# Value products of a local attention: two heads' turned probabilities as weights, values streamed beside zeros

## The chip, the cores and the metric

One core of a Trainium2 chip. The metric is the device time of one execution in microseconds: 4424.85 us in the median of three runs (4423.68 to 4428.69).

## The reference, cut to what matters

The layer has two branches, whose outputs are added: a delta-rule attention (not touched), and a transformer of six layers on 16 sequences of 256 tokens with 128 channels. A layer of the transformer is local attention and a gated feed-forward block:

```python
DIM = 128; DEPTH = 6; HEADS = 16; DIM_HEAD = 64; WINDOW = 32

def local_attention(q, k, v):
    # windows of 32 queries, each against its own and the preceding window's keys
    bk2, bv2 = look(bk), look(bv)                      # (b, h, 8, 64, 64)
    sim = jnp.einsum('bhwie,bhwje->bhwij', bq, bk2) * QK_SCALE
    sim = jnp.where(mask, -jnp.finfo(sim.dtype).max, sim)
    attn = jax.nn.softmax(sim, -1)                     # 32 queries x 64 keys
    out = jnp.einsum('bhwij,bhwje->bhwie', attn, bv2)  # the value products
    return out.reshape(b, h, n, d)
# attn_layer: q, k, v = x @ Wqkv; l2norm and rotary on q, k; local_attention; @ Wo
# ffn_layer: layernorm; a, gate = split(x @ W1 + b1); (a * gelu(gate)) @ W2 + b2
```

Everything is float32. The sequences are independent of each other; within one, a layer needs the layer before.

## The kernel before, in words

`local_transformer` is a software pipeline written out by hand. A body is one pass of it and works on five sequences (items) at once, each a stage further: `new` (projection of queries and keys, 8 chunks), `turn` (scaling, transposes to head-major form, the value projection), `att` (scores, softmax, first value products), `out` (last value products, output projection, layer norm statistics) and `ffn`. 16 bodies make a layer, 96 the transformer, and four more empty it. Each engine has its own `body(b)`: the list of calls there is the order in which that engine executes, and semaphores (`need(engine, semaphore, count)`) hold it to its inputs and to the buffers that come free. An engine never goes past a call that waits. There is no planner: to move work is to move a line of such a list.

- The state is kept turned (channels on partitions, tokens in columns). A projection is three float32r products of 512 columns (`project`, L1402) into the one bank `ps_proj`; VectorE rotates it (L1228, L1235), ScalarE squares it (`square`, L1066), and the next projection waits for that square. GpSimd adds and scales, TensorE transposes (`turn_qk`, L1437).
- `score(x, k)` handles 8 heads of one half of the sequence (128 tokens): a mask product (L1448), then 32 products of a 64-row by 32-column weight with 64 streamed columns (L1454). In float32 each product is two records.
- `turn_probs` transposes the normalised probabilities (L1469). `pT` then has, for two heads r, 64 keys each on the partitions and the queries in the columns.
- `weigh(x, k)` (L1487) makes the value products: for 4 pairs of heads, 4 windows and 2 heads, a 64 x 64 block of values is the weight and the 32 columns of that head's probabilities are streamed. The result is already turned (value channel on partitions), and ScalarE copies it into `oT` (`heads_out`, L1115), from which `join_heads` makes the output projection.
- The values: `value(b, x, n)` projects four parts into `ps_p`, ScalarE copies them into `v` (`value_out`, L1088; tokens on partitions, one buffer). A window needs its own keys and those of the window before on one set of 64 partitions. `window(x)` on SP (L935) therefore copies `v` into `vw`, inside SBUF, with 16 DMAs a sequence, after the fourth part is in `v`. `vw` has two buffers. `value_out` of the next sequence's part 0 waits until all 16 have landed, since it overwrites `v`.
- The layer norm of `ffn` shares VectorE's Newton steps for the inverse square roots with `turn`'s norms (`inverse_roots`), at the start of a body.

Of the kernel before, what the change touches and what calls it, by code (L numbers as in the profile page):

```python
# [11 lines left out]
ALU = mybir.AluOpType  # L12
# [15 lines left out]
UNITS = 4  # L28
NNORM = 64
NPREP = 10  # L30
# [770 lines left out]
def local_transformer(nc, stateT, ident, wqkv_d, scales_d, wb_d, par_d, rot_d, mask_d):  # L801
# [8 lines left out]
    with ExitStack() as stack:  # L810
        def sb(name, shape, dt=F32):
# [18 lines left out]
        ident_r = sb("ident_r", [P, P], F32R)  # L830
# [15 lines left out]
        vw = sb("vw", [P, 2, NWIN, INNER // 2])  # L846
# [5 lines left out]
        oT = sb("oT", [P, 2, NPAIR, L])  # L852
# [5 lines left out]
        hid = sb("hid", [P, FCH, L])  # L858
# [9 lines left out]
            "vw_in0", "vw_in1",  # L868
            "scored", "maxed", "shifted", "exped", "p_summed", "reciped", "normed", "p_turned", "p_turned_out",
            "valued", "values_out", "wo_done", "x_added", "xf_ready", "mean_done", "centred",  # L870
# [36 lines left out]

        block = stack.enter_context(nc.Block())

        @block.sync  # L910
        def _(sp):
            sp.dma_start(par_all[:, :], par_d).then_inc(S["loaded_const"], 16)
            sp.dma_start(rot_base[:, :, :], rot_d.rearrange("(u p) n -> p u n", p=P)).then_inc(S["loaded_const"], 16)
            sp.dma_start(hid[:, :, :].rearrange("p c t -> p (c t)")[:, 0:2 * KEYS], mask_d).then_inc(S["loaded_const"], 16)
# [8 lines left out]
            def window(x):  # L923

                if not x.there:
                    return
                need(sp, S["v_out"], x.u * 4 + 4)
                for r in range(2):
                    for a in range(2):
                        rows = slice(r * KEYS + a * WIN, r * KEYS + (a + 1) * WIN)  # L930
                        cols = slice(r * CK, (r + 1) * CK)
                        for c in range(4):
                            n = 1 if a == 0 and c == 3 else 2
                            w = c + 1 - a
                            sp.dma_start(vw[rows, x.q, w:w + 4 * (n - 1) + 1:4, :], v[c * WIN:(c + 1) * WIN, 0:n, cols])\  # L935
                                .then_inc(S[f"vw_in{x.q}"], 16)

            def body(b):
                new, turn, att, out, ffn = b.items
                window(att)  # L940
# [8 lines left out]
            load_wqkv(0)  # L949
            pipeline(body)  # L950

        @block.gpsimd
        def _(pool):

            nc.gpsimd.memset(kT[:, :, :, 0:WIN], 0.0).then_inc(S["prepared"], 1)
            nc.gpsimd.memset(vw[:, :, 0, :], 0.0).then_inc(S["prepared"], 1)
# [6 lines left out]
            nc.gpsimd.tensor_copy(ident_r[:, :], ident[:, :]).then_inc(S["prepared"], 1)  # L963

            pool.wait_ge(S["loaded_const"], 48)
            nc.gpsimd.tensor_copy(mask[:, :, :], hid[:, :, :].rearrange("p c t -> p (c t)")[:, 0:2 * KEYS]
# [42 lines left out]
            def body(b):  # L1009
                new, turn, att, out, ffn = b.items  # L1010
                if turn.there:
# [3 lines left out]
                scale(att, 7)  # L1015
                scale(turn, 0)
                scale(turn, 1)
                add(turn, 7)
                add(new, 0)
                scale(turn, 2)  # L1020
                add(new, 1)
                scale(turn, 3)
                norm(out, 3)
                scale(turn, 4)
                add(new, 2)
                norm(att, 0)
                add(new, 3)
                norm(att, 1)
                scale(turn, 5)
                add(new, 4)  # L1030
                add(new, 5)
                norm(att, 2)
                scale(turn, 6)
                add(new, 6)
# [4 lines left out]
        def _(act):  # L1039
# [41 lines left out]
            def value_out(x, before, n):  # L1081
# [4 lines left out]
                if n == 0:  # L1086
                    need(act, S[f"vw_in{before.q}"], 256 * (before.h + 1))
# [20 lines left out]

            def heads_out(x, k):

                if not x.there:
                    return
                half, e = unit(k)
                need(act, S["valued"], x.u * 4 + (k + 1))
                nc.scalar.activation(oT[:, x.q, 4 * e:4 * e + 4, half * P:(half + 1) * P],  # L1115
                                     ps_o[:, :].rearrange("p (c t) -> p c t", c=4), ACT.Copy).then_inc(S["values_out"], 1)
# [34 lines left out]
            def body(b):  # L1151
                new, turn, att, out, ffn = b.items
                shift_state(ffn)
                square(turn, 6)
                heads_out(out, 0)
                probs_out(out, 1)
                turned_out(att, 5)
                square_centred(ffn)
                value_out(att, out, 3)
                if b.switch == -1:  # L1160
                    convert(b, (4, 5), (S["v_projected"], turn.u * 4))
                square(turn, 7)
# [8 lines left out]
                turned_out(att, 6)  # L1171
                heads_out(out, 1)
                probs_out(out, 2)
                turned_out(att, 7)
                square(new, 0)
                turned_out(turn, 0)
                heads_out(out, 2)
# [6 lines left out]
                square(new, 2)  # L1184
                value_out(turn, att, 0)
                probs_out(out, 3)
                exp(att, 0)
                square(new, 3)
                turned_out(turn, 3)
                exp(att, 1)  # L1190
                heads_out(out, 3)
                value_out(turn, att, 1)
                turned_out(turn, 4)
                square(new, 4)
                probs_out(att, 0)
                square(new, 5)
                exp(att, 2)
                value_out(turn, att, 2)
                if b.switch == 1:
                    need(act, S["y_done"], ffn.u + 1)  # L1200
                    nc.scalar.activation(w1[:, :, :, :].rearrange("p a c n -> p (a c n)"), stage_w1, ACT.Copy)\
                        .then_inc(S["conv_act"], 1)

# [3 lines left out]
        def _(dve):  # L1207
            dve.wait_ge(S["loaded_const"], 48)
# [101 lines left out]
            def hidden(x):  # L1310
# [5 lines left out]
                for c, bank in enumerate((ps_g[:, L:2 * L], ps_c[:, 0:L], ps_c[:, L:2 * L])):  # L1316
                    nc.vector.scalar_tensor_tensor(hid[:, c, :], bank, par[:, c:c + 1], gate[:, c, :], ALU.add, ALU.mult)\
# [10 lines left out]
            def body(b):  # L1328
                new, turn, att, out, ffn = b.items
                centre(ffn)  # L1330
                rotate(turn, 7, 0)
                rotate(turn, 7, 1)
                sum_squares(turn, 7)
                inverse_roots(turn, ffn)
# [10 lines left out]
                top(out, 3)  # L1345
                rotate(new, 0, 1)
                if b.switch == -1:
                    convert(b, (4, 5), 4)
                deviate(ffn)
                shift(out, 3)  # L1350
                sum_squares(new, 0)
                rotate(new, 1, 0)
                rotate(new, 1, 1)
                total(out, 3)
                sum_squares(new, 1)
                top(att, 0)
                rotate(new, 2, 0)
                shift(att, 0)
                rotate(new, 2, 1)
                top(att, 1)  # L1360
                hidden(ffn)
                rotate(new, 3, 0)
                sum_squares(new, 2)
                rotate(new, 3, 1)
                shift(att, 1)
                total(att, 0)
                sum_squares(new, 3)
                rotate(new, 4, 0)
# [8 lines left out]
                total(att, 1)  # L1377
# [3 lines left out]
                top(att, 2)  # L1381
                shift(att, 2)
# [7 lines left out]
                sum_squares(new, 6)  # L1390

# [3 lines left out]
        def _(pe):  # L1395
# [77 lines left out]
            def weigh(x, k):  # L1473
# [5 lines left out]
                need(pe, S["values_out"], x.u * 4 + k)  # L1479
                if k == 0:  # L1480
                    need(pe, S[f"vw_in{x.q}"], 256 * (x.h + 1))
                for c in range(NPAIR // 2):
                    for w in range(4):
                        for r in range(2):
                            rows = slice(r * KEYS, (r + 1) * KEYS)
                            first = (4 * e + c) * DH
                            mm = nc.tensor.matmul(ps_o[rows, c * P + w * WIN:c * P + (w + 1) * WIN],  # L1487
                                                  vw[rows, x.q, 4 * half + w, first:first + DH],
                                                  pT[rows, k % 2, c, w * WIN:(w + 1) * WIN],
                                                  start=True, stop=True, skip_group_check=True)  # L1490
                mm.then_inc(S["valued"], 1)

            def join_heads(b, x):
# [7 lines left out]
                for c in range(NPAIR):  # L1501
                    mm = nc.tensor.matmul(ps_c[:, 0:L], wo[:, c, :], oT[:, x.q, c, :], start=c == 0, stop=c == NPAIR - 1)  # L1502
# [29 lines left out]
            def ffn_in(x, part):  # L1532
# [3 lines left out]
                need(pe, S["xn_ready"], x.u + 1)  # L1536
                if part == 2:
# [6 lines left out]
            def ffn_out(x):  # L1544
# [4 lines left out]
                for c in range(FCH):  # L1549
                    mm = nc.tensor.matmul(ps_c[:, 0:L], w2[:, c, :], hid[:, c, :], start=c == 0, stop=c == FCH - 1)  # L1550
                mm.then_inc(S["y_done"], 1)

            def body(b):
                new, turn, att, out, ffn = b.items
                query_key(b, new, 0)
                turn_qk(att, 7)
                weigh(out, 2)
                spread(ffn)
                turn_qk(turn, 0)
                score(att, 0)  # L1560
                query_key(b, new, 1)
                turn_qk(turn, 1)
                ffn_in(ffn, 0)
                ffn_in(ffn, 1)
                value(b, turn, 0)
                query_key(b, new, 2)
                turn_qk(turn, 2)
                score(att, 1)
                ffn_in(ffn, 2)
                turn_qk(turn, 3)  # L1570
                query_key(b, new, 3)
                turn_probs(out, 3, turn, 0)
                ffn_out(ffn)
                weigh(out, 3)
                query_key(b, new, 4)
                value(b, turn, 1)
                turn_qk(turn, 4)
                score(att, 2)
                turn_probs(att, 0, turn, 1)
                query_key(b, new, 5)  # L1580
                join_heads(b, out)
                turn_qk(turn, 5)
                query_key(b, new, 6)
                value(b, turn, 2)
                weigh(att, 0)
                turn_probs(att, 1, turn, 2)
# [3 lines left out]
                mean(out)  # L1590
                query_key(b, new, 7)
                value(b, turn, 3)
                variance(out)
                turn_qk(turn, 6)
                turn_probs(att, 2, turn, 3)
                weigh(att, 1)
                score(att, 3)
# [148 lines left out]
```

## Time and profile before

| | |
|---|---|
| median of three runs | 4424.85 us |
| the profiled execution | 4430.44 us, span 4428.3 us |
| PE / weight loads, share of the span | 90% / 76% |
| VectorE / ScalarE / GpSimd | 77% / 56% / 52% |
| mean granted clock of TensorE | 0.929 |
| the transformer | from about 725 us to 4409 us |

"PE" is TensorE's products, "PEld" its weight loads, DVE VectorE, ACT ScalarE, POOL GpSimd, SP the engine that issues the DMAs. A row of windows has the stretch, its length, and the busy us (and instructions) of PE, PEld, DVE, ACT and POOL, then TensorE's granted clock, the busy share of the 16 DMA engines, and GB/s. The time before 725 us is the other branch, which the change leaves alone. Busy shares of the whole span mix it in; a layer or a body of the transformer says more.

### The profile page before, as it was taken

To read this page: it belongs to the slowest core of one execution; us is meant where nothing else is said; L and a number is where in the kernel's file an instruction comes from. 1 tells how busy PE (TensorE), PEld (TensorE's weight loads), DVE (VectorE), ACT (ScalarE), POOL (GpSimd) and SP (SyncE) were. 2 spreads that over 40 slices of the span, in tenths; PEclk is the share of its full clock that TensorE was granted. 3 is DMA by queue.
4 is the path that set the end of the run, shared out by engine and by line. 5 is a ranking of instruction groups with operands and counts; after the bars stand their busy time and mean duration, and the time that the engine had idled before them with its cause. 6 is when DMAs were issued, how large, how long until landed. Compare 5 with 4: busy or idle time off the path is not lost. (4 is left out here: it accounts for less than half of the span.)

```text
span 4428.3 us, 165233 instructions
## 1 busy us (share of the span) xinstructions
PE 4003.8 (90%) x71312; PEld 3348.1 (76%) x71312; DVE 3420.2 (77%) x6567; ACT 2492.3 (56%) x4423; POOL 2303.8 (52%) x2141
## 2 busy tenths in 40 slices
PE   4746743899999999999999999999999999999997
PEld 4635531688888888878888888888788888888885
DVE  4376565788888888888888888888888888888883
ACT  2322211466666666666666666666666666666663
POOL 1000002566656666666666666666666665666661
PEclk9766655899999999999999999999999999999998
DMA  1000000222222222222222222222222222222222
GB/s 57 22 12 12 2 12 34 71 56 56 56 56 57 71 56 57 56 57 71 56 56 56 56 66 71 56 56 56 66 71 56 56 56 53 64 55 57 53 57 64
DMA packets 133868, 232.99 MB, mean 53 GB/s; under 512 B 26640, under 2 KB 36624, under 8 KB 131472
## 3 DMA queue, kind: packets, MB, share of 16 engines
q1 hardware_dynamic: 133136, 222.32, 20.6%
q8 instruction: 571, 9.36, 1.0%
q14 instruction: 161, 1.32, 0.1%
HBM read 29.28 MB, written 4.19 MB: 8 GB/s over the span
## 5 line engine op out<-in xcount | busy, mean ns | idle before, releaser
L987 POOL TENSOR_TENSOR qk<-rot_a,rot_b 128x512 f32<-128x512 f32 x768 | 983.5, 1285 | 418.7 <-PE bank L1437 378.2
L997 POOL TENSOR_TENSOR qk<-qk,rn 128x512 f32<-128x512 f32 x768 | 801.5, 1049 | 216.0 <-DVE rn L69 206.1
L1487 PEld LDWEIGHTS bank<-pT,vw 64*64 64x64 f32 x24576 | 752.3, 136 | 100.5 <-issue 99.5
L1487 PE MATMUL bank<-pT,vw 64*64 64x32 f32 x24576 | 794.9, 220 | 0.7 <-ACT pT L1106 0.7
L1006 POOL TENSOR_TENSOR pr<-pr,prec 128x512 f32<-128x512 f32 x384 | 400.2, 1042 | 706.1 <-DVE prec L1272 705.9
L1228 DVE TENSOR_TENSOR rot_a<-bank,rot 128x512 f32<-128x512 f32 x768 | 529.4, 689 | 297.6 <-PE bank L1402 296.4
L1066 ACT ACTIVATE sq<-bank 128x512 f32<-128x512 f32 x768 | 457.5, 596 | 470.4 <-DVE rot_b L1235 465.0
L1402 PE MATMUL bank<-w_hi,xs_hi 128*128 128x512 f32 x1152 | 555.3, 482 | 77.7 <-ACT sq L1066 28.2
L1243 DVE TENSOR_REDUCE ss<-sq 128x8 f32<-128x512 f32 x768 | 509.6, 664 | 139.0 <-ACT sq L1066 139.0
L1235 DVE TENSOR_TENSOR rot_b<-bank,rot 128x512 f32<-128x512 f32 x768 | 522.9, 681 | 0.0
L1437 PE MATMUL bank<-ident,qk 128*128 128x128 f32 x3072 | 472.6, 277 | 4.9 <-POOL qk L997 4.7
L1402 PE MATMUL bank<-w_hi,xs_lo 128*128 128x512 f32 x1152 | 461.8, 401 | 0.0
L1402 PE MATMUL bank<-w_lo,xs_hi 128*128 128x512 f32 x1152 | 460.5, 400 | 0.0
L1454 PEld LDWEIGHTS bank<-kT,qT 64*32 64x32 f32 x24576 | 363.5, 107 | 116.8 <-issue 116.7
L1437 PEld LDWEIGHTS bank<-ident,qk 128*128 128x128 f32 x3072 | 386.1, 145 | 81.5 <-POOL qk L997 9.3
L1454 PE MATMUL bank<-kT,qT 64*32 64x64 f32 x24576 | 426.9, 219 | 1.2 <-issue 0.9
L1088 ACT ACTIVATE v<-bank 128x512 f32<-128x512 f32 x384 | 229.1, 597 | 278.3 <-PE bank L1402 274.2
L1502 PE MATMUL bank<-oT,wo 128*128 128x256 f32 x1536 | 347.2, 379 | 0.7 <-ACT oT L1115 0.7
L1106 ACT ACTIVATE pT<-bank 128x512 f32<-128x512 f32 x384 | 229.2, 597 | 192.2 <-PE bank L1469 192.2
L1077 ACT ACTIVATE kT<-bank 128x512 f32<-128x512 f32 x384 | 228.1, 594 | 191.9 <-PE bank L1437 191.2
L1402 PEld LDWEIGHTS bank<-w_hi,xs_hi 128*128 128x128 f32 x1152 | 221.2, 192 | 137.0 <-issue 52.1
L1502 PEld LDWEIGHTS bank<-oT,wo 128*128 128x128 f32 x1536 | 291.5, 190 | 43.3 <-ACT oT L1115 0.8
(238 smaller groups left out, 6724.6 us busy)
## 6 DMA issues: line engine op xcount, KB each, us to landing
vw<-v SPq DMA_DIRECT2D x1344, 128.0 KB
vw<-v SPq DMA_DIRECT2D x192, 64.0 KB
stage<-in_wqkv SPq DMA_DIRECT2D x6, 1536.0 KB, 6.1
stage<-in_wb_all SPq DMA_DIRECT2D x6, 1088.0 KB, 5.3
d_band<-in_band SPq DMA_DIRECT2D x8, 512.0 KB, 5.3
d_xt<-in_x SPq DMA_DIRECT2D x4, 512.0 KB, 4.1
base_scratch<-d_res SPq DMA_DIRECT2D x4, 512.0 KB, 3.0
o_base<-base_scratch SPq DMA_DIRECT2D x1, 2048.0 KB, 8.4
```

The costliest lines, as they stand in the source:

```text
L987: nc.gpsimd.tensor_tensor(qk[:, c, :], rot_a[:, c % 2, :], rot_b[:, c % 2, :], ALU.add)\
L997: nc.gpsimd.tensor_tensor(y, y, rn[:, x.q, 8 * c:8 * c + 8].unsqueeze(2).to_broadcast([P, 8, DH]), ALU.mult).then_inc(S["scaled"], 1)
L1006: nc.gpsimd.tensor_tensor(y, y, prec[:, k % 2, :].unsqueeze(2).to_broadcast([P, NPAIR, KEYS]), ALU.mult).then_inc(S["normed"], 1)
L1066: nc.scalar.activation(sq[:, :], ps_proj[:, :], ACT.Square).then_inc(S["squared"], 1)
L1228: nc.vector.tensor_tensor(rot_a[:, c % 2, :].rearrange("p (h d) -> p h d", h=8), ps_proj[:, :].rearrange("p (h d) -> p h d", h=8), cos, AL ...
L1235: nc.vector.tensor_tensor(rot_b[:, c % 2, :].rearrange("p (h a d) -> p h a d", h=8, a=2), y[:, :, ::-1, :], sin, ALU.mult).then_inc(S["rot ...
L1243: nc.vector.tensor_reduce(ss[:, 8 * c:8 * c + 8], sq[:, :].rearrange("p (h d) -> p h d", h=8), AX.X, ALU.add).then_inc(S["summed"], 1)
L1402: mm = nc.tensor.matmul(out[:, :], x[:, q, half * P:(half + 1) * P], w[:, cols:cols + CK], start=n == 0, stop=n == 2)
L1437: mm = nc.tensor.transpose(ps_turn[:, i * P:(i + 1) * P], qk[:, c, i * P:(i + 1) * P], ident[:, :])
L1454: mm = nc.tensor.matmul(bank[w * WIN:(w + 1) * WIN, h * KEYS:(h + 1) * KEYS], qT[rows, x.q, h, q0:q0 + WIN], kT[rows, x.q, h, q0:q0 + KEYS ...
L1487: mm = nc.tensor.matmul(ps_o[rows, c * P + w * WIN:c * P + (w + 1) * WIN], vw[rows, x.q, 4 * half + w, first:first + DH], pT[rows, k % 2, ...
L1502: mm = nc.tensor.matmul(ps_c[:, 0:L], wo[:, c, :], oT[:, x.q, c, :], start=c == 0, stop=c == NPAIR - 1)
```

## The change

The value products swap their operands. The turned probabilities of two heads (128 partitions, 32 queries) become the weight, and the values of the two heads are streamed, 128 columns: head 0's values stand in the first 64 columns on the first 64 partitions, head 1's in the last 64 on the other 64, and the rest of `vw` is zero, written once by VectorE. A product gives 32 queries by two heads of 64 channels; the four windows go to the four groups of 32 output partitions. There are 16 products a call and not 32. The output now has tokens on partitions: ScalarE copies it to `o_tok` (`heads_taken`), TensorE transposes it into `ps_g` (`turn_heads`, four transposes a call, four calls a sequence), ScalarE copies that to `oT` (`heads_out`).

`vw` becomes a ring of three halves. `window(x, half)` issues 14 DMAs for the first half and 16 for the second, each of 32 partitions by 2 KB. It is called for `turn`, no longer for `att`: the first half waits for v's second part, the second for v's fourth and for the products that read the slot before. `value_out(turn, att, 0)` waits for both halves of `att`.

All five orders are written anew. `inverse_roots`, `centre`, `shift_state` and `square_centred` move to the end of the body before, `score(x, 0)` too. `oT` has one buffer, `hid` is written in place of `gate`.

```diff
+SLOTS = 3
+HALF_DMAS = (14, 16)
-        vw = sb("vw", [P, 2, NWIN, INNER // 2])
+        vw = sb("vw", [P, SLOTS, NWIN // 2, 2, CK])
-        oT = sb("oT", [P, 2, NPAIR, L])
+        o_tok = sb("o_tok", [P, CK])
+        oT = sb("oT", [P, NPAIR, L])
+        def slot(x, half):
+            return (2 * x.u + half) % SLOTS
@@ SP
-            def window(x):
+            def window(x, half):
-                need(sp, S["v_out"], x.u * 4 + 4)
+                need(sp, S["v_out"], x.u * 4 + 2 * half + 2)
+                need(sp, S["valued"], x.u * 4 + 2 * half - 4)
                 for r in range(2):
                     for a in range(2):
                         rows = slice(r * KEYS + a * WIN, r * KEYS + (a + 1) * WIN)
                         cols = slice(r * CK, (r + 1) * CK)
-                        for c in range(4):
-                            n = 1 if a == 0 and c == 3 else 2
-                            w = c + 1 - a
-                            sp.dma_start(vw[rows, x.q, w:w + 4 * (n - 1) + 1:4, :], v[c * WIN:(c + 1) * WIN, 0:n, cols])
+                        for w in range(4):
+                            n, c = (half, w) if a == 1 else (half, w - 1) if w else (half - 1, 3)
+                            if n >= 0:
+                                sp.dma_start(vw[rows, slot(x, half), w, r, :], v[c * WIN:(c + 1) * WIN, n, cols])
-                window(att)
+                window(turn, 0)
+                window(turn, 1)
@@ ScalarE, its body up to square(new, 3), without the layer switches
+                high_half(b, new)
+                value_out(att, out, 3)
+                probs_out(out, 2)
+                heads_taken(out, 1)
+                turned_out(att, 7)
+                heads_taken(out, 2)
+                heads_out(out, 1)
+                square(new, 0)
+                turned_out(turn, 0)
+                affine(ffn)
+                exp(out, 3)
+                heads_out(out, 2)
+                value_out(turn, att, 0)
+                turned_out(turn, 1)
+                square(new, 1)
+                gelu(ffn)
+                square(new, 2)
...
@@ VectorE
+            nc.vector.memset(vw[:, :, :, :, :], 0.0).then_inc(S["vw_zeroed"], 1)
@@ TensorE
-                        for r in range(2):
-                            rows = slice(r * KEYS, (r + 1) * KEYS)
-                            first = (4 * e + c) * DH
-                            mm = nc.tensor.matmul(ps_o[rows, c * P + w * WIN:c * P + (w + 1) * WIN],
-                                                  vw[rows, x.q, 4 * half + w, first:first + DH],
-                                                  pT[rows, k % 2, c, w * WIN:(w + 1) * WIN],
+                        first = (4 * e + c) * DH
+                        mm = nc.tensor.matmul(ps_o[w * WIN:(w + 1) * WIN, c * P:(c + 1) * P].rearrange("p (r d) -> p r d", r=2),
+                                              pT[:, k % 2, c, w * WIN:(w + 1) * WIN],
+                                              vw[:, slot(x, half), w, :, first:first + DH],
+            def turn_heads(x, k):
+                need(pe, S["o_out"], x.u * 4 + (k + 1))
+                need(pe, S["values_out"], x.u * 4 + k)
+                if k == 3:
+                    need(pe, S["hid_done"], (x.u - 1) * 3 + 1)
+                for c in range(NPAIR // 2):
+                    mm = nc.tensor.transpose(ps_g[:, c * P:(c + 1) * P], o_tok[:, c * P:(c + 1) * P], ident[:, :])
@@ TensorE, the new order of its body, calls of one line joined
+                query_key(b, new, 0); turn_heads(out, 1); weigh(out, 2); spread(ffn); value(b, turn, 0)
+                turn_qk(turn, 0); turn_heads(out, 2); query_key(b, new, 1); score(att, 1); turn_qk(turn, 1)
+                ffn_in(ffn, 1); ffn_in(ffn, 0); query_key(b, new, 2); turn_qk(turn, 2)
+                turn_probs(out, 3, turn, 0); score(att, 2); ffn_in(ffn, 2); query_key(b, new, 3)
+                value(b, turn, 1); turn_qk(turn, 3); ffn_out(ffn); weigh(out, 3); turn_qk(turn, 4)
+                query_key(b, new, 4); turn_probs(att, 0, turn, 1); turn_qk(turn, 5); turn_heads(out, 3)
+                weigh(att, 0); query_key(b, new, 5); join_heads(b, out); query_key(b, new, 6)
+                value(b, turn, 2); turn_heads(att, 0); mean(out); turn_qk(turn, 6)
+                turn_probs(att, 1, turn, 2); query_key(b, new, 7); score(att, 3); value(b, turn, 3)
+                variance(out); turn_qk(turn, 7); weigh(att, 1); turn_probs(att, 2, turn, 3); score(turn, 0)
```

## Rows read from the trace of the kernel before

**Rows 1.** Windows: a layer, then one body; columns as told above.
```profile
2058.00:2646.00 588.00, 582.72 (x10153) 490.26 (x10146) 489.75 (x953) 381.09 (x685) 375.26 (x349) 0.99 0.26 61
2406.19:2442.99 36.80, 36.80 (x646) 31.04 (x645) 30.65 (x61) 24.01 (x43) 23.55 (x22) 1.00 0.25 59
```
**Rows 2.** Groups by shape: line, engine, tile, shapes, count, then busy us, mean ns.
```profile
L1487 PE MATMUL bank<-pT,vw 64*64 64x32 f32 x24576 | 794.9, 220 | 0.7 <-ACT pT L1106 0.7
L1454 PE MATMUL bank<-kT,qT 64*32 64x64 f32 x24576 | 426.9, 219 | 1.2 <-issue 0.9
```
**Rows 3.** Timeline of TensorE in one body: start us, us, line.
```profile
2408.65 0.71 PE L1527 MATMUL bank<-ident,rn 128*128 128x128 f32 x4
2409.20 0.60 PE L1437 MATMUL bank<-ident,qk 128*128 128x128 f32 x4
...
2412.21 1.89 PE L1541 MATMUL bank<-xn,w 128*128 128x256 f32 x8
2413.75 0.58 PE L1402 MATMUL bank<-w_hi,xs_hi 128*128 128x512 f32 x1
...
2436.60 0.40 PE L1402 MATMUL bank<-w_hi,xs_hi 128*128 128x512 f32 x1
...
2437.29 0.57 PE L1518 MATMUL bank<-mean_w,xsq 128*128 128x1 f32 x4
2437.72 0.63 PE L1437 MATMUL bank<-ident,qk 128*128 128x128 f32 x4
2438.24 0.63 PE L1469 MATMUL bank<-ident,pr 128*128 128x128 f32 x4
2438.79 2.06 PE L1487 MATMUL bank<-pT,vw 64*64 64x32 f32 x64
2440.78 0.39 PE L1448 MATMUL bank<-mask,ident_b 128*128 128x512 bf16 x1
2441.10 1.10 PE L1454 MATMUL bank<-kT,qT 64*32 64x64 f32 x64
2442.13 0.50 PE L1402 MATMUL bank<-w_hi,xs_hi 128*128 128x512 f32 x1
```
**Rows 4.** Timeline of ScalarE: v's part 3, a square, and v's next part 0.
```profile
2400.70 0.60 ACT L1088 ACTIVATE v<-bank 128x512 f32<-128x512 f32 x1 [0.29 <-PE bank L1402]
...
2409.69 0.60 ACT L1066 ACTIVATE sq<-bank 128x512 f32<-128x512 f32 x1 [2.32 <-DVE rot_b L1235]
...
2417.94 0.59 ACT L1088 ACTIVATE v<-bank 128x512 f32<-128x512 f32 x1
```
**Rows 5.** SP's issues at L935, duration ns min/median/max: the whole run, then one burst.
```profile
L935 SPq DMA_DIRECT2D vw<-v x1536: 585/598/2278, 793.7 to 4352.4; - x192
...
L935 SPq DMA_DIRECT2D vw<-v x16: 586/598/1617, 2401.3 to 2412.6; - x16
```
**Rows 6.** DMA issues by size, whole run.
```profile
vw<-v SPq DMA_DIRECT2D x192, 64.0 KB
```
**Rows 7.** Window: the last microsecond of that burst.
```profile
2415.00:2416.00 1.00, 1.00 (x8) 0.62 (x6) 0.71 (x2) 0.99 (x4) 1.00 (x2) 1.00 0.07 16
```
**Rows 8.** Timeline of VectorE: the last Newton step of a body.
```profile
2407.63 0.23 DVE L69 SCALAR_TENSOR_TENSOR rn<-rn_t,rn 128x66 f32<-128x66 f32 x1
```
**Rows 9.** Timeline of TensorE where a layer changes.
```profile
1319.47 0.77 PE L1402 MATMUL bank<-w_hi,xs_hi 128*128 128x512 f32 x1 [4.45 <-issue]
```
**Rows 10.** Windows around two changes of layer.
```profile
1315.00:1320.00 5.00, 0.55 (x4) 0.50 (x2) 4.90 (x7) 0.95 (x2) 4.42 (x5) 0.57 0.68 157
1320.00:1325.00 5.00, 5.00 (x67) 4.33 (x65) 3.82 (x6) 1.19 (x2) 1.54 (x2) 0.50 0.60 137
1325.00:1330.00 5.00, 5.00 (x85) 4.17 (x84) 1.61 (x3) 2.21 (x4) 2.27 (x2) 0.56 0.01 3
...
2520.00:2525.00 5.00, 4.75 (x67) 4.05 (x67) 4.61 (x7) 0.95 (x2) 2.32 (x2) 0.60 0.72 167
```
**Rows 11.** Waits, whole run: who waited for whom, us in total, times, longest.
```profile
PE bank L1402 <- issue: 18.2, 5, 4.5
```

More of the change, by code:

```diff
@@ L906, in unit, with landed @@
             return k // 2, k % 2
+        def slot(x, half):
+            return (2 * x.u + half) % SLOTS
+        def landed(x, half):
+            k = 2 * x.u + half
+            return 16 * sum(HALF_DMAS[i % 2] for i in range(k % SLOTS, k + 1, SLOTS))
         block = stack.enter_context(nc.Block())
@@ L1010, in body @@
                 new, turn, att, out, ffn = b.items
-                if turn.there:
+                if out.there:
+                    low_half(new, "normed", out.u * 4 + 3)
+                elif att.there:
+                    low_half(new, "scaled", att.u * 8 + 8)
+                elif turn.there:
                     low_half(new, "added", turn.u * 8 + 7)
@@ L1014, in body @@
                     low_half(new, "prepared", NPREP)
-                scale(att, 7)
                 scale(turn, 0)
+                add(turn, 7)
                 scale(turn, 1)
-                add(turn, 7)
                 add(new, 0)
+                norm(out, 3)
                 scale(turn, 2)
+                scale(turn, 3)
                 add(new, 1)
-                scale(turn, 3)
-                norm(out, 3)
                 scale(turn, 4)
+                scale(turn, 5)
                 add(new, 2)
@@ L1027, in body @@
                 add(new, 3)
-                norm(att, 1)
-                scale(turn, 5)
                 add(new, 4)
                 add(new, 5)
+                scale(turn, 6)
+                norm(att, 1)
+                add(new, 6)
+                scale(turn, 7)
                 norm(att, 2)
-                scale(turn, 6)
-                add(new, 6)
             pipeline(body)
@@ L1085, in value_out @@
                 need(act, S["v_projected"], x.u * 4 + (n + 1))
-                if n == 0:
-                    need(act, S[f"vw_in{before.q}"], 256 * (before.h + 1))
+                if n == 0 and before.there:
+                    need(act, S[f"vw_in{slot(before, 0)}"], landed(before, 0))
+                    need(act, S[f"vw_in{slot(before, 1)}"], landed(before, 1))
                 nc.scalar.activation(v[:, n // 2, n % 2 * CK:(n % 2 + 1) * CK], ps_p[:, :], ACT.Copy)\
@@ L1107, in probs_out, with heads_taken @@
                     .then_inc(S["p_turned_out"], 1)
+            def heads_taken(x, k):
+                if not x.there:
+                    return
+                need(act, S["valued"], x.u * 4 + (k + 1))
+                need(act, S["o_turned"], x.u * 4 + k)
+                nc.scalar.activation(o_tok[:, :], ps_o[:, :], ACT.Copy).then_inc(S["o_out"], 1)
             def heads_out(x, k):
@@ L1113, in heads_out @@
                 half, e = unit(k)
[L1114 to L1116 removed]
+                need(act, S["o_turned"], x.u * 4 + (k + 1))
+                nc.scalar.activation(oT[:, 4 * e:4 * e + 4, half * P:(half + 1) * P],
+                                     ps_g[:, :].rearrange("p (c t) -> p c t", c=4), ACT.Copy).then_inc(S["values_out"], 1)
             def shift_state(x):
@@ L1152, in body @@
                 new, turn, att, out, ffn = b.items
[L1153 to L1162, printed above, removed]
                 if b.switch == -2:
@@ L1182, in body @@
                 gelu(ffn)
+                square(new, 2)
                 turned_out(turn, 2)
-                square(new, 2)
-                value_out(turn, att, 0)
                 probs_out(out, 3)
                 exp(att, 0)
+                turned_out(turn, 3)
+                value_out(turn, att, 1)
                 square(new, 3)
-                turned_out(turn, 3)
-                exp(att, 1)
[L1191 to L1195, printed above, removed]
+                turned_out(turn, 4)
+                heads_taken(out, 3)
+                probs_out(att, 0)
+                square(new, 4)
+                heads_out(out, 3)
+                exp(att, 1)
+                exp(att, 2)
                 square(new, 5)
-                exp(att, 2)
+                turned_out(turn, 5)
+                heads_taken(att, 0)
+                shift_state(out)
                 value_out(turn, att, 2)
@@ L1202, in body @@
                         .then_inc(S["conv_act"], 1)
+                square(new, 6)
+                probs_out(att, 1)
+                heads_out(att, 0)
+                square_centred(out)
+                turned_out(turn, 6)
+                square(new, 7)
             pipeline(body)
@@ L1344, in body @@
                 rotate(new, 0, 0)
-                top(out, 3)
+                shift(out, 3)
                 rotate(new, 0, 1)
@@ L1380, in body @@
                 rotate(new, 5, 1)
-                top(att, 2)
-                shift(att, 2)
+                total(att, 1)
                 sum_squares(new, 5)
@@ L1390, in body @@
                 sum_squares(new, 6)
+                centre(out)
+                rotate(new, 7, 0)
+                rotate(new, 7, 1)
+                top(att, 3)
+                sum_squares(new, 7)
+                inverse_roots(new, out)
             pipeline(body)
@@ L1536, in ffn_in @@
                 need(pe, S["xn_ready"], x.u + 1)
+                if part == 0:
+                    need(pe, S["values_out"], min(x.u * 4 + 7, UNITS * NSEQ * DEPTH))
                 if part == 2:
@@ L1549, in ffn_out @@
                 for c in range(FCH):
-                    mm = nc.tensor.matmul(ps_c[:, 0:L], w2[:, c, :], hid[:, c, :], start=c == 0, stop=c == FCH - 1)
+                    mm = nc.tensor.matmul(ps_c[:, 0:L], w2[:, c, :], gate[:, c, :], start=c == 0, stop=c == FCH - 1)
                 mm.then_inc(S["y_done"], 1)
@@ L1555, in body @@
                 query_key(b, new, 0)
-                turn_qk(att, 7)
+                turn_heads(out, 1)
                 weigh(out, 2)
                 spread(ffn)
+                value(b, turn, 0)
                 turn_qk(turn, 0)
-                score(att, 0)
+                turn_heads(out, 2)
                 query_key(b, new, 1)
+                score(att, 1)
                 turn_qk(turn, 1)
+                ffn_in(ffn, 1)
                 ffn_in(ffn, 0)
-                ffn_in(ffn, 1)
-                value(b, turn, 0)
                 query_key(b, new, 2)
                 turn_qk(turn, 2)
-                score(att, 1)
+                turn_probs(out, 3, turn, 0)
+                score(att, 2)
                 ffn_in(ffn, 2)
+                query_key(b, new, 3)
+                value(b, turn, 1)
                 turn_qk(turn, 3)
-                query_key(b, new, 3)
-                turn_probs(out, 3, turn, 0)
                 ffn_out(ffn)
                 weigh(out, 3)
+                turn_qk(turn, 4)
                 query_key(b, new, 4)
-                value(b, turn, 1)
-                turn_qk(turn, 4)
-                score(att, 2)
                 turn_probs(att, 0, turn, 1)
+                turn_qk(turn, 5)
+                turn_heads(out, 3)
+                weigh(att, 0)
                 query_key(b, new, 5)
                 join_heads(b, out)
-                turn_qk(turn, 5)
                 query_key(b, new, 6)
                 value(b, turn, 2)
-                weigh(att, 0)
-                turn_probs(att, 1, turn, 2)
+                turn_heads(att, 0)
                 if b.switch == 1:
@@ L1590, in body @@
                 mean(out)
+                turn_qk(turn, 6)
+                turn_probs(att, 1, turn, 2)
                 query_key(b, new, 7)
+                score(att, 3)
                 value(b, turn, 3)
                 variance(out)
-                turn_qk(turn, 6)
+                turn_qk(turn, 7)
+                weigh(att, 1)
                 turn_probs(att, 2, turn, 3)
-                weigh(att, 1)
-                score(att, 3)
+                score(turn, 0)
             pipeline(body)
```

63 lines of the change are left out of this document (28 added, 35 removed).

## Prediction

> **What bounds the kernel now.** I read the windows first. A layer of 588 us has TensorE busy for 582.7 us, and one body of the pipeline, 36.80 us, has it busy without a break, with VectorE at 30.65, ScalarE at 24.01 and GpSimd at 23.55 us [rows 1]. So in the transformer TensorE's written order sets the pace, and an edit there is worth what it does to a body, times 96 (16 sequences, 6 layers). Next the groups by shape: the value products are 24,576 records (each fp32 product is two), with 795 us on PE [rows 2]. Then TensorE's own timeline of a body, for what each block takes from its start to the next one's: weigh 1.99 us, the mask and the score products 0.32 + 1.03, a group of four transposes 0.52 or 0.55 (I take 0.5), value 0.69, variance 0.43, spread 0.55, the two first feed-forward calls 1.54 [rows 3]. Last the queue of SP, because each body copies v into vw: ScalarE finishes v's fourth part at 2401.30, SP starts its 16 issues at once, the last starts at 2412.6, and in the window 2415 to 2416 the DMA engines are nearly quiet (share 0.07). The burst takes 13.8 us. ScalarE overwrites v at 2417.94, so 16.6 us were allowed and nothing waited [rows 4, 5, 7]. That is a cover of 2.8 us which no list of waits shows.
>
> **TensorE's work.** A weigh is now 32 records with 32-column weights (a window's probabilities of two heads) and 128 streamed columns. The nearest row is the score: 64 records, 32-column weights, 64 streamed columns, four column positions, 1.03 us. Both stream 4,096 columns, so 1.03 again, 1.05 with the change of tiles. Saved: 4 x (1.99 - 1.05) = 3.8 us a body. Added are four turn_heads of four transposes, 4 x 0.5 = 2.0 us. A body falls from 36.8 to 35.0 us if TensorE stays the bound. Bounds for a weigh: 1.0 (as the score), and 4.3, if nothing overlaps: 32 x (0.11 to stream 128 columns, as the variance's four 128-column loads stand 0.11 apart and four 128-column transposes 0.13, + 0.03 for a load of 32).
>
> The row of the score shows what decides here: its 64 loads and products all use one half of the rows, differ only in their column position, and take 1.03 us, 16 ns each, where one 64-column stream alone needs about 54 (half of 0.11). The loads and streams of four column positions therefore run beside each other. The Trainium skill ("TensorE: Matmul & The Clock Gate", Part 3: Packing small matmuls) says that a weight load overlaps products in flight only when the row group differs. By that, the new weigh, which uses all rows each time, would be serial. The trace speaks against the rule.
>
> **ScalarE and VectorE.** heads_taken adds four copies of 0.60 us a body: 24.0 + 2.4 = 26.4 of 35.0, hidden beside TensorE. VectorE keeps its work: 30.65 of 35.0. The new order puts inverse_roots at the end of its body. Its chain from the last projection to the last Newton step ended at 2407.86, 0.8 us before spread [rows 3, 8]. In the new order TensorE passes score 3, value, variance, turn, weigh, turn, score 0, projection, turn_heads and weigh in between: 1.35 + 0.7 + 0.43 + 0.5 + 1.05 + 0.5 + 1.35 + 0.7 + 0.5 + 1.05 = 8.1 us, against the chain's 7.9. Hidden, barely; some tenths a body if late. hid folded into gate, oT with one buffer, the waits for ps_g (values_out, hid_done): I walked the order, and the awaited copies come some tenths ahead; zero. VectorE's memset of vw, 12,288 columns (a 512-column pass takes 0.69), is at most 14 us once beside the load of the weights; zero, at most 3 us.
>
> **The copies of v, where the gain is lost.** window is moved to the item `turn`, and split in halves of 14 and 16 DMAs of 64 KB. The first half leaves in mid-body; it has a body of time. The second waits for v_out of part 3, which ScalarE does early in the next body, and for weigh(att, 1). Behind it stands ScalarE's value_out(turn, att, 0), which overwrites v, and in ScalarE's queue behind that turned_out(turn, 1) and square(new, 1). query_key(new, 2) on TensorE needs that square.
>
> What TensorE has to do between the end of weigh(att, 1) and query_key 2: turn_probs 0.5, score 1.35, projection 0.7, turn_heads 0.5, weigh 1.05, spread 0.55, value 0.7, turn 0.5, turn_heads 0.5, projection 0.7, score 1.35, turn 0.5, feed-forward 1.55 = 10.45 us. What the other way takes: 16 issues and the landing, then three ScalarE operations of 0.60 with their handovers, 1.85, and 0.05 to start.
> - The burst's bounds: the issue of a vw DMA takes 598 ns in the median and never under 585, among 1,536 of which 192 move 64 KB [rows 5, 6]. Halving the bytes doesn't make it cheaper. The floor is 15 x 0.6 = 9.0 us plus the 2.5 from the last issue to quiet, 11.5. The top is 13.8, as now; the excess is single issues of up to 2.3 us. Whether these come by the count or the bytes the trace doesn't say, so I take the middle, 13.0.
> - TensorE's gap before query_key 2: 13.0 + 1.9 - 10.45 = 4.4 us (2.9 to 5.2). The body is 35.0 + 4.4 = 39.4 us, or 37.9 to 40.2: at either end over 36.8. The same 16 issues as before stand behind the last part of v, but the order now allows them 10 us and not 16.6.
>
> **The clock.** Where a layer changes, TensorE stands still for up to 4.45 us (18.2 us in five gaps). With the gap that ends at 1319.47 the granted clock falls to half (0.57 over 1315 to 1320), is 0.50 for the next five, 0.56 over 1325 to 1330: 9.9 us of cold work. In 2520 to 2525 it is 0.60, some 3.8 us of work [rows 9 to 11]. The middle is 6.8 us, which lose half of it, 3.4. A gap of 4.4 us in each body is of that size. I take it that three bodies in four pay: 2.6 us. A body is then 42.0 us.
>
> **Sum.** (42.0 - 36.8) x 96 = +499 us. The profiled execution took 4430.4 us (span 4428.3 and 2.1 around it), 5.6 over the runs' median, 4424.85. 4430 + 499 - 5.6 = 4924, say 4925 us.
>
> **Rivals.**
> - *The gap comes but the clock holds.* The gaps shown stand at layer changes only, and a body may differ. (39.4 - 36.8) x 96 = +250: 4675 us.
> - *The copies are in time, the kernel is faster.* If the bytes decide, half of them land in half of 13.8, 6.9 us, against an allowance of 10.45 - 1.9 = 8.5. TensorE stays the bound: (35.0 - 36.8) x 96 = -173: 4252 us. It decides from a burst under 10.3 us (gap under 1.8), issues of 0.52. For it: every added piece fits under TensorE. Against: the 64 KB issues [rows 5, 6]. The Trainium skill ("DMA: Bandwidth & Descriptors", Issuing engines are not separate DMA queues) calls the sequencer's time to start a DMA usually small relative to the DMA. Here the issues are 11.3 of 13.8 us, so this case's rows contradict it.
> - *Between them:* a burst near 10.3, within some per cent of 4425 either way.
> - *The new products don't overlap:* 4.3 us a weigh, TensorE 35.0 + 4 x 3.25 = 48.0; one of them lies in the burst's cover (13.7), which leaves a gap of 1.2: 49.2 us, +1190: 5610 us. The score's row speaks against it.
>
> **Chances.** Forecast 0.45, clock holds 0.30, in time 0.16, between 0.05 (of it 0.01 faster, 0.02 same, 0.02 slower), no overlap 0.04. Within 0.2% (9 us) is what a measurement here can't tell from no change. Faster 0.17, same 0.02, slower 0.81. The range leaves out "in time" and "no overlap": below, 4400; above, every body cold (42.8 us, 5001) and the gap at 5.2 (+0.8 x 96 = 77), about 5090. Slower alone, it is 4530 (floor of the burst, warm clock: +1.1 x 96) to 5090.
>
> **What would show it.** A wait of ScalarE's v on the vw DMAs of some 4 us in every body; TensorE's gap before the projection behind the feed-forward pair; SP's 30 issues a body at a median near 598 ns; a granted clock well under 0.99 over a layer; weigh near 1.05 us. Wrong, if issues of the new form take 0.5 us or less, if the landing follows the bytes, or if ScalarE gets to value_out more than 13 us after weigh(att, 1) for a reason of its own, since then the copies cost nothing extra.

## The result and the profile after

4744.54 us in the median of four runs (4728.2 to 4751.3) against 4426.77 us, the median of four runs of the kernel before; the ratio is 1.0712 (95% interval 1.0683 to 1.0742). The change makes the kernel 7% slower, though TensorE has less to do. The profiled execution took 4728.20 us with a span of 4726.1: 297.8 us more than before, 3.1 us for each of 96 bodies.

Windows of the changed kernel: the stretch of a layer, and one body; the columns are those of [rows 1].

```profile
2055.00:2680.00 625.00, 558.19 (x8166) 450.69 (x8165) 463.72 (x928) 403.71 (x732) 365.35 (x340) 0.95 0.21 54
2403.61:2445.35 41.74, 36.50 (x536) 29.36 (x534) 29.70 (x61) 25.93 (x47) 23.58 (x23) 0.92 0.20 49
```

TensorE was busy without a break in the body of [rows 1]. Here it stands still for 5.24 of the body's 41.74 us. Its timeline, as [rows 3]:

```profile
2407.46 1.08 PE L1514 MATMUL bank<-vw,pT 128*32 128x128 f32 x32
2408.47 0.66 PE L1498 MATMUL bank<-ident,pr 128*128 128x128 f32 x4
...
2417.32 1.89 PE L1582 MATMUL bank<-xn,w 128*128 128x256 f32 x8
2424.46 0.79 PE L1431 MATMUL bank<-w_hi,xs_hi 128*128 128x512 f32 x1 [5.24 <-ACT sq L1081]
```

The new weigh (the first line) takes 1.01 us to the next block, where the old one took 1.99. The gap stands before query_key 2, behind the feed-forward pair, and what ends it is a square on ScalarE. ScalarE's timeline, as [rows 4]:

```profile
2407.68 0.60 ACT L1104 ACTIVATE v<-bank 128x512 f32<-128x512 f32 x1
...
2422.83 0.60 ACT L1104 ACTIVATE v<-bank 128x512 f32<-128x512 f32 x1 [6.06 <-DMA vw<-v]
2423.32 0.59 ACT L1092 ACTIVATE kT<-bank 128x512 f32<-128x512 f32 x1
2423.80 0.60 ACT L1081 ACTIVATE sq<-bank 128x512 f32<-128x512 f32 x1
```

v's part 3 is there at 2408.28, and the block behind weigh(att, 1) starts at 2408.47. Both are what the second half's copies wait for. Yet v is overwritten only at 2422.83, 14.4 us later. In [rows 4] the same copy waited for nothing. The square that TensorE needs is two places behind it. Over the whole run these two are the longest waits of their engines (us, times, longest):

```profile
ACT v L1104 <- DMA vw<-v: 437.5, 95, 6.5
...
PE bank L1431 <- ACT sq L1081: 383.4, 107, 6.0
```

SP's issues, as [rows 5]:

```profile
L946 SPq DMA_DIRECT2D vw<-v x2880: 507/591/2059, 774.6 to 4650.9; - x192
DMA to landing us min/median/max: 1.9/2.0/3.5
```

All 2,880 move 64 KB, and the median issue takes 591 ns, where 598 ns was the median with mostly 128 KB. Half the bytes buy 7 ns. The granted clock around the gap, in windows as in [rows 10]:

```profile
2415.00:2419.00 4.00, 4.00 (x80) 3.05 (x78) 3.35 (x7) 1.74 (x4) 2.71 (x3) 1.00 0.36 87
2419.20:2424.50 5.30, 0.06 (x2) 0.05 (x1) 0.06 (x1) 1.65 (x4) 4.39 (x5) 0.71 0.20 51
2424.50:2430.00 5.50, 5.50 (x80) 4.31 (x81) 3.19 (x5) 4.93 (x8) 1.27 (x1) 0.66 0.00 0
```

It is full (1.00, 2.4 GHz) up to the gap and falls in it. The 0.66 over the 5.5 us behind the gap means 3.7 us at 1.2 GHz. Of 95 bodies, 79 have such a stretch within 12 us behind the gap, and the layer's mean is 0.95 where it was 0.99.

### The profile page after: what moved, and what is told of

Same layout as the page of the kernel before. It is cut to its first block and busy times, and to the rows that moved or that the text cites. A ratio compares the mean times of both kernels' runs of the same rounds, so it can differ in the third digit from the quotient of the medians.

```text
span 4726.1 us, 146508 instructions
## 1 busy us (share of the span) xinstructions
PE 3936.3 (83%) x60560; PEld 3171.3 (67%) x60560; DVE 3352.1 (71%) x6568; ACT 2672.4 (57%) x4807; POOL 2302.0 (49%) x2139
## 5 line engine op out<-in xcount | busy, mean ns | idle before, releaser
L1431 PE MATMUL bank<-w_hi,xs_hi 128*128 128x512 f32 x1152 | 585.3, 508 | 425.7 <-ACT sq L1081 383.4
L1466 PE MATMUL bank<-ident,qk 128*128 128x128 f32 x3072 | 507.7, 291 | 8.3 <-ACT kT L1092 6.0
L1431 PE MATMUL bank<-w_lo,xs_hi 128*128 128x512 f32 x1152 | 474.3, 412 | 0.0
L1483 PEld LDWEIGHTS bank<-kT,qT 64*32 64x32 f32 x24576 | 388.6, 113 | 125.8 <-issue 125.8
L1431 PE MATMUL bank<-w_hi,xs_lo 128*128 128x512 f32 x1152 | 471.6, 409 | 0.0
L1483 PE MATMUL bank<-kT,qT 64*32 64x64 f32 x24576 | 451.7, 226 | 0.0
L1514 PE MATMUL bank<-vw,pT 128*32 128x128 f32 x12288 | 417.9, 277 | 0.2 <-ACT pT L1122 0.2
L1514 PEld LDWEIGHTS bank<-vw,pT 128*32 128x32 f32 x12288 | 314.1, 110 | 81.3 <-issue 64.5
L1131 ACT ACTIVATE o_tok<-bank 128x512 f32<-128x512 f32 x384 | 229.1, 597 | 214.9 <-PE bank L1514 214.9
```

The costliest lines, as they stand in the source:

```text
L1431: mm = nc.tensor.matmul(out[:, :], x[:, q, half * P:(half + 1) * P], w[:, cols:cols + CK], start=n == 0, stop=n == 2)
L1466: mm = nc.tensor.transpose(ps_turn[:, i * P:(i + 1) * P], qk[:, c, i * P:(i + 1) * P], ident[:, :])
L1483: mm = nc.tensor.matmul(bank[w * WIN:(w + 1) * WIN, h * KEYS:(h + 1) * KEYS], qT[rows, x.q, h, q0:q0 + WIN], kT[rows, x.q, h, q0:q0 + KEYS ...
L1514: mm = nc.tensor.matmul(ps_o[w * WIN:(w + 1) * WIN, c * P:(c + 1) * P].rearrange("p (r d) -> p r d", r=2), pT[:, k % 2, c, w * WIN:(w + 1) ...
```

## The experiments

**Two buffers for v.** If the wait for the burst of copies costs the time, a second buffer must give it back: part 0 of the next sequence then goes into the other half of `v` and waits for the copies of the sequence before last. To make room, the DMA scratch is set to 1024 bytes. All else stays.

```diff
-        v = sb("v", [P, 2, INNER])
+        v = sb("v", [P, 2, 2, INNER])                        # by the sequence's parity
...                                                           (v[:, x.q, ...] where v is written and read)
-                if n == 0 and before.there:                   # both halves of x.u - 1
+                if n == 0 and before.there and before.u > 0:  # both halves of x.u - 2
+                    for k in (2 * x.u - 4, 2 * x.u - 3):
+                        need(act, S[f"vw_in{k % SLOTS}"], 16 * sum(...))   # sum cut
-... dynamic_dma_scratch_size=8192)
+... dynamic_dma_scratch_size=1024)
```

> The changed kernel with v in two buffers (by the sequence's parity), so that value_out(turn, att, 0) waits for the copies of the sequence before last. Theory (the second half's burst of 16 issues holds v, and through square(new, 1) TensorE): ScalarE's wait on the vw DMAs goes, TensorE's gap of 3.8 us goes, the clock stays full; a body takes 34.6 to 35.0 us: 4220 to 4260 us. Rival (the swapped products, the transposes behind them or the new order cost the time themselves): it stays above 4600 us, with the gap at another place.

Measured: 4196.09 us, ratio to the kernel before 0.9468 (0.9451 to 0.9486). This version beats both kernels. Its body:

```profile
2442.00:2476.10 34.10, 34.10 (x532) 28.06 (x532) 30.04 (x61) 25.88 (x47) 23.14 (x23) 1.00 0.22 54
```

TensorE has no idle time in it, and the clock is full. From one mean(out) to the next (2463.34 to 2497.80) are 34.46 us, where [rows 1] has 36.80. So the swapped products, the transposes and the new order together are worth 2.34 us a body, and the changed kernel loses all of that and more by having one buffer. A control with the scratch alone:

> A control for the kernel with two buffers of v, which also asks for 1024 bytes of DMA scratch and not 8192 to make room: the changed kernel with that edit alone. Theory: no DMA of this kernel goes through it; 4728 to 4751 us. Rival (the scratch was part of the gain): under 4700.

Measured: 4721.34 us. That is one run, 7 us under the lowest of the changed kernel and just outside what was expected. The gaps are there as before, so the scratch has no part worth naming in the 548 us between one buffer and two.

**Half the DMAs, half the bytes, twice the DMAs.** These three vary the count of the issues and the bytes. In the first, `for r in range(2 - half)`: the 8 copies of head row 1 are left out of a second half. In the second, each copy of a second half takes only `0:CK // 2` of its columns, and the rest of the values isn't copied. In the third, each copy of a second half is issued as two of half the columns.

> The changed kernel with 8 of the 16 DMAs of a second half left out (those of head row 1; part of the values stays zero), each still 64 KB. Theory by issues: 8 x 0.6 + 2.5 = 7.3 us, under the 8.5 that are allowed; the gap goes, 4220 to 4280 us. Theory by bytes: half the bytes, also in time, 4220 to 4280. Neither: about 4740 us.

> The changed kernel with all 16 DMAs of a second half, each of 32 KB and not 64 (half of the values' columns isn't copied). Theory by issues: 16 x 0.6 + 2.3 = 11.9 us or more, gap 2.8 to 3.5 us; 4640 to 4745 us. Theory by bytes: half the burst, the gap goes, 4220 to 4280 us.

> The changed kernel with each DMA of a second half split into two of half the columns: 32 issues for the same bytes. Theory by issues: 16 more x 0.6 = 9.6 us more in each body's gap (13.4 us), and no less cold work behind it: 5650 to 5900 us. Theory by bytes: as the changed kernel, about 4740 us.

Measured: 4200.88, 4719.65 and 5748.18 us, one run each. With 8 issues, ScalarE's copies into v waited 1.5 us for DMAs in the whole run. Its waits in the second and third:

```profile
ACT v L1105 <- DMA vw<-v: 404.2, 95, 6.1
```
```profile
ACT v L1106 <- DMA vw<-v: 1372.8, 95, 16.9
```

8 issues are in time. 16 are late even with half the bytes (4.3 us a body, where the changed kernel has 4.6). 16 more issues for the same bytes cost ScalarE 9.8 us a body more, 0.61 us each. So it is the count of the issues that limits the burst, and the theory by bytes is out.

**Filling the gap.** The gap costs twice, by itself and by the halved clock behind it. Products whose result nobody reads keep TensorE busy in part of the gap and so show the second cost alone.

```diff
                 ffn_in(ffn, 0)
+                filler(out)   # 12 bf16 products of 512 columns into ps_o, after o_out of k = 2
                 query_key(b, new, 2)
```

> The changed kernel with 12 idle products more in each body, bf16, 512 columns, into the bank ps_o, which is free there, right before query_key(new, 2), where TensorE stands still for 3.8 us: 12 x 0.22 = 2.6 us of work nobody reads. Theory (the gap costs twice, once by itself and once by the halved clock behind it, 3.5 us of cold work a body, half of it lost): the rest of the gap, 1.2 us, leaves the clock up; 1.8 us a body less, about 4575 us (4560 to 4620). Rival (cold work lies in another wait's shadow): 4740 us, or above where a gap was under 2.6 us.

Measured: 4613.80 us (4599.9 to 4618.6), ratio to before 1.0414 (1.0388 to 1.0440). With 12 more products in each body the kernel is 131 us faster than the changed one. In the same stretch the clock is now full, and TensorE's idle time before the projection is down from 383.4 us:

```profile
2055.00:2680.00 625.00, 596.22 (x8690) 468.11 (x8689) 482.87 (x967) 417.64 (x760) 375.96 (x350) 1.00 0.22 57
```
```profile
PE bank L1432 <- ACT sq L1082: 151.2, 103, 6.3
```

So the halved clock costs 1.4 us a body at the least (6 of 95 bodies had a gap under 2.6 us, and in those the filler itself costs). The gain of 1.8 us that was expected was a little too high.

**Moving the wait** instead of removing it.

```diff
@@ ScalarE
                 heads_out(out, 2)
-                value_out(turn, att, 0)
                 turned_out(turn, 1)
...
                 turned_out(turn, 2)
+                value_out(turn, att, 0)
@@ TensorE
-                turn_probs(out, 3, turn, 0)
                 score(att, 2)
                 ffn_in(ffn, 2)
+                turn_probs(out, 3, turn, 0)
```

> The changed kernel with one buffer of v as it is; only two calls move: value_out(turn, att, 0) on ScalarE goes from before turned_out(turn, 1) to behind turned_out(turn, 2), and turn_probs(out, 3) on TensorE from before score(att, 2) to behind ffn_in(ffn, 2). Theory (what costs is the place of value_out, 10.6 us of TensorE's work behind the burst's start where 14.5 are needed): query_key 2 and 3, their transposes, a score and the feed-forward call come into the cover, 3.4 us more; the gap falls to 0 to 0.8 us, the clock stays up; 4200 to 4290 us. Rival (SP's burst costs wherever the wait stands): 4700 or more.

Measured: 4356.01 us, ratio to before 0.9837 (0.9814 to 0.9860): faster than both kernels with v in one buffer, but 66 us above the range expected. ScalarE no longer waits for the copies (7.1 us in all). In their place TensorE has two waits of half a microsecond in each body:

```profile
PE bank L1591 <- DVE gate L1346: 53.5, 95, 2.0
PE bank L1498 <- ACT v L1104: 53.3, 106, 2.9
```

This idle time is 1.1 us a body, and the kernel stands 1.7 us a body above the one with two buffers. Measured from the start of one block to the start of the next, the two places cost 0.69 and 0.71 us in the body at 2400 us, which is most of the 1.7. The first wait is that of the feed-forward's last product for its input; why that input is late is not traced. The second follows from the edit: `turn_probs(out, 3)` writes the bank from which `value_out(turn, att, 0)` copies, so it waits for the very copy that was moved back.

**Two queues.** ScalarE issues the 8 DMAs of head row 1 behind its value_out(att, out, 3).

```diff
+                copy_row_1(att)    # nc.scalar.dma_start x8, after v_out of part 3 and weigh(att, 1)
```

> The changed kernel, v in one buffer, with the second half's burst shared: SP issues the 8 DMAs of head row 0, ScalarE the 8 of head row 1, right behind its value_out(att, out, 3). The copies are in time either way (8 x 0.6 + 2.5 = 7.3 us). If an issue holds ScalarE as it holds SP (0.6 us), 4.8 us stand before probs_out(out, 2) and heads_taken(out, 1), for which TensorE has some 1.5 us; it stands still there for 2 to 3 us a body: 4430 to 4600 us. If an issue costs ScalarE next to nothing: 4200 to 4260 us. If SP's queue as such was not the limit: 4740.

Measured: 4825.95 us in one run, beyond the range. The copies are in time now (no wait of v on them is left), but ScalarE's timeline shows what they cost there:

```profile
2402.76 5.39 ACTq L1116 DMA_DIRECT2D vw<-v  x8
2408.25 0.60 ACT L1134 ACTIVATE pT<-bank 128x512 f32<-128x512 f32 x1 [5.88 <-issue]
```
```profile
PE bank L1542 <- ACT o_tok L1143: 359.5, 77, 6.4
```

An issue holds ScalarE as it holds SP, 0.67 us each. The gap moves to turn_heads(out, 1). There it is 4.7 us (the mean of 77 between 900 and 4100 us of the run), where 2 to 3 were expected, and the mean clock falls from the changed kernel's 0.902 to 0.878.

**Column positions of the products** (on the kernel with two buffers): `for w in range(4)` is put outside of the loop over the four pairs, so eight records in a row go to the same 32 columns of the array.

> The kernel with two buffers of v (4196 us), and in weigh the loop over windows outside of the loop over pairs: eight records in a row go to one position of 32 columns, where they went to four in turn. The same products. Theory (the 1.01 us of a weigh come from four column positions at once): in one position the streams follow each other, 32 x 0.11 = 3.5 us a weigh, +2.5 x 4 a body: 5150 us (5100 to 5250). With loads that overlap nothing either, 4.4 us a weigh: 5500. Rival (each record costs 32 ns wherever it goes, or TensorE reorders them itself): 4200 us.

Measured: 4696.08 us in one run, between the two forecasts. The call takes 2.46 us where it took 1.08 by the same row:

```profile
2408.56 2.46 PE L1514 MATMUL bank<-vw,pT 128*32 128x128 f32 x32
```

The theory's direction holds: the same 32 records take 2.3 times as long when eight in a row share a position. Its size doesn't. Within a position they stand 0.11 us apart, as expected. But the next window's run of eight starts 0.47 us after the one before, beside its fifth record, so that about one and a half positions are busy on average.

**The kernel before, with its burst in 30 issues.** Each 128 KB copy becomes two of 64 KB; the counts that are waited for follow, and are not shown.

```diff
-  sp.dma_start(vw[rows, x.q, w:w + 4 * (n - 1) + 1:4, :], v[c * WIN:(c + 1) * WIN, 0:n, cols])
+  for m in range(n):
+      sp.dma_start(vw[rows, x.q, w + 4 * m, :], v[c * WIN:(c + 1) * WIN, m, cols])
```

> The kernel before, with each 128 KB DMA of a burst issued as two of 64 KB: 30 issues for the same bytes. Theory: the burst takes 30 x 0.62 + 2 = 20.6 us where 16.6 us are allowed; ScalarE waits some 4 us in each body, TensorE 3 to 3.5, and the clock falls behind it: 4.5 to 5 us a body, 4860 to 4920 us. Rival (only the bytes count, and 2.8 us are left as now): 4430 us.

Measured: 5138.15 us in one run, 708 us more than before for the same bytes, and more than expected.

```profile
ACT v L1089 <- DMA vw<-v: 537.8, 90, 9.5
...
PE bank L1470 <- ACT v L1089: 482.3, 90, 8.3
```

The wait is 6.0 us and not 4. From the first issue to the copy that overwrites v it is 22.9 us in the mean, where the estimate was 20.6: an issue takes 0.71 us in the mean and not 0.62 (2.8 of a burst take over 1 us). As many rows of 2 KB are moved as before, so SP's time doesn't go by rows either, but by issues. In the body of [rows 4] and [rows 5] the kernel before was 2.8 us from the same loss, with no wait that showed it.

## Why the prediction was right

The direction, the mechanism and the place were right, and 4744.5 us lies in the range (4400 to 5090). The forecast of +499 us was 1.6 times the 318 measured; the largest part of the difference, 0.9 us a body, is in the term of the clock. By its steps:

- *TensorE's work, 36.8 to 35.0 us a body.* 34.46 us in the kernel with two buffers. weigh is 1.01 us (1.05 forecast), a turn_heads 0.35 to 0.53 (0.5). The 4252 us of the rival with the copies in time were a little cautious; 4196 is what that gives. The row of the score decided this rightly. By the rule of the Trainium skill ("TensorE: Matmul & The Clock Gate", Part 3: Packing small matmuls) the new weigh would be serial; its weights are on all rows, and 32 records at four column positions still take 1.01 us, 32 ns each. (The bound without any overlap, 32 x 0.14, is 4.5 us and not 4.3.)
- *The cover, 10.45 us of TensorE's work behind weigh(att, 1).* 10.7 us in the body shown (2408.47 to the end of the feed-forward pair at 2419.2), and in the median.
- *The burst, 13.0 us, and the gap, 4.4.* The burst was right: from its first issue to its last landing it takes 12.9 us in the mean of the bodies (11.8 to 14.1). The handovers behind it take 1.7 us and not 1.9, and the cover is 0.2 us longer, which makes the usual gap 4.1. TensorE's idle time before this projection is 383.4 / 96 = 4.0 us a body, with the 28.2 us that the same row had before, so 3.7 us were added. Whether issues beyond 1 us come by the count or by the bytes was left open. They follow neither: 203 of 2,880 last over 1 us here, 203 of 2,880 with half the bytes, and 207 of 4,416 with the DMAs of a second half doubled.
- *The clock, 2.6 us a body.* The term most off: 1.4 (the gain of the filler, a lower bound) to 1.7. Counted over the trace, TensorE works 610 us at 1.2 GHz, and 285 us in the kernel with two buffers (the other branch is in both). That is 3.4 us more in a body, of which half is lost, 1.7. The forecast took the middle of the cold stretches at changes of layer, 6.8 us, for three bodies in four. The share of bodies was about right; the stretches are shorter, 3.7 us in the body shown.
- The sum of what was measured: -2.34 + 3.7 + 1.7 = +3.06 us a body, against 3.1. No other term is needed. VectorE's chain before spread, the waits for ps_g and the added ScalarE copies were put at zero; nothing in the two-buffer kernel's TensorE waits speaks against it. Zeroing vw took VectorE 10.3 us, once, and nobody waited for it (by the prediction's own row, 24 x 0.69, the bound was 16.6 us and not 14).
- The rival "the clock holds" gave 4675 us, nearer to the time than the forecast. That is luck: its gap is too large and its saving on TensorE too small, which offsets in part that the clock does fall.

## What to carry to other kernels

Ask of each transfer that frees a buffer how long the order allows it and how long it takes, also where no wait is shown: the kernel before had 2.8 us to spare and the change took 6. A burst of DMAs as small as these (32 to 128 KB) from one queue costs by its count, and halving the bytes saved ScalarE 0.3 us of a wait of 4.6. Fewer, larger copies shorten the burst (16 of up to 128 KB take 13.8 us where 30 of 64 KB take 22.9), and a second buffer (8 KB a partition here) removes the wait. Where TensorE must wait some microseconds once in a body, count the work at the halved clock behind the gap too: products that nobody reads, put into the gap, can be cheaper than the bare gap.

## What the hardware showed that I had not expected

- Some issues of these copies take 1 to 2.3 us, where the median is 0.59 or 0.60. Their number follows neither the count nor the bytes: besides the three figures above, it is 211 of 1,536 in the kernel before and 266 of 2,880 with its burst in 30 issues. The cause stays open.
- 12 bf16 products of 512 columns added to each of 96 bodies made the kernel 131 us faster: the granted clock over a layer is 1.00 with them and 0.95 without.
- Runs of eight fp32 records (128 columns streamed, 32-column weights) at one column position still take 77 ns each, less than their stream of 109, since the next window's run starts beside them; in turn over four positions they take 32 ns.
